# Triangle attention and triangle multiplication on one core: the output gate's constants move from POOL to PE, and the bias rows of the projections into four row tiles

## What is computed

```python
x = x + L0(gn(x))       # triangle attention, 4 heads
x = x + L1(gn(x))       # triangle multiplication
```

```python
zn   = layernorm(z) * ln_in_w + ln_in_b
a    = mask * sigmoid(zn @ a_g_w.T + a_g_b) * (zn @ a_p_w.T + a_p_b)
b    = mask * sigmoid(zn @ b_g_w.T + b_g_b) * (zn @ b_p_w.T + b_p_b)
t    = einsum('bikh,bjkh->bijh', a, b)
tn   = layernorm(t) * ln_out_w + ln_out_b
gate = sigmoid(zn @ g_w.T + g_b)
out  = gate * (tn @ z_w.T + z_b)
```

## Time and profile before

| | |
|---|---|
| median of 3 runs | 285.29 us (284.13 to 285.58) |
| the profiled execution | 284.4 us, span 282.6 us |
| mean granted clock of PE | 0.886 |
| busy | PE 80%, PE weight loads 65%, DVE 75%, ACT 74%, POOL 51% |

### The profile page before, as it was taken

How to read it: one execution, slowest core, us unless ns; L and a number is a source line. 1 busy time by engine, 2 the same in 40 slices (tenths; PEclk the granted TensorE clock), 3 DMA queues, 4 the chain that set the end, 5 groups by cost and what they waited for, 6 DMA issues and landing times.

```text
span 282.6 us, 6859 instructions
## 1 busy us (share of the span) xinstructions
PE 226.4 (80%) x2394; PEld 182.6 (65%) x2394; DVE 210.6 (75%) x368; ACT 209.2 (74%) x953; POOL 144.4 (51%) x132
## 2 busy tenths in 40 slices
PE   0589492469999999999999999999669599677930
PEld 0579230347888878888788887888459566376930
DVE  4047962357999999999999999998545739959790
ACT  0566643279999999999999999999545645569590
POOL 5400000008876777767777677766200019998081
PEclk9999668579999999999999999999958689965695
DMA  8400033534454643554445553330000000000038
GB/s 130 63 11 2 1 112 121 171 124 142 145 171 170 221 163 132 199 181 165 165 149 195 184 186 118 117 115 2 0 2 0 0 2 2 1 1 2 0 49 118
DMA packets 42389, 27.09 MB, mean 96 GB/s; under 512 B 24404, under 2 KB 42356, under 8 KB 42356
## 3 DMA queue, kind: packets, MB, share of 16 engines
q1 hardware_dynamic: 36572, 25.95, 28.8%
q10 hardware_dynamic: 5784, 0.71, 1.7%
HBM read 1.36 MB, written 1.18 MB: 9 GB/s over the span
## 4 chain that ended last, share of the span: by engine, by line
PE 31%; issue 27%; ACT 21%; DVE 12%; POOL 4%; SPq 3%; POOLq 1%; DMA 0%; DVEq 0%; ACTq 0%
ACT maps L659 17%; PE psum L1181 7%; PE psum L1060 3%; PE psum L1192 3%; PE psum L1145 2%; SPq L392 2%; DVE u_full L951 2%; PE psum L1248 2%; PE psum L1171 2%; DVE shared L991 2%; PE psum L1226 2%; PE psum L1231 2%; PE psum L1146 1%; PE psum L1148 1%; PE psum L1257 1%
## 5 line engine op out<-in xcount | busy, mean ns | idle before, releaser
L659 ACT ACTIVATE maps<-psum,neg_max 96x96 f32<-96x96 f32 x384 | 123.9, 353 | 4.9 <-DVE neg_max L928 4.1
L490 POOL TENSOR_TENSOR maps<-maps,rden 96x768 f32<-96x768 f32 x48 | 70.5, 1469 | 81.5 <-DVE rden L938 75.3
L659 ACT ACTIVATION_READ_ACCUMULATOR maps<-psum,neg_max 96x1 f32 x384 | 83.9, 219 | 0.0
L944 DVE COPY turned<-psum 96x1024 f32<-96x1024 f32 x48 | 58.5, 1219 | 8.4 <-PE psum L1181 8.4
L928 DVE TENSOR_REDUCE neg_max<-psum 96x8 f32<-96x768 f32 x48 | 45.7, 953 | 5.1 <-PE psum L1148 4.9
L1145 PE MATMUL psum<-u_st,x_stack 128*96 128x384 f32 x96 | 37.8, 394 | 10.4 <-DVE bias_lo L913 8.1
L1181 PE MATMUL psum<-ident,maps 96*96 96x96 f32 x384 | 40.0, 247 | 0.3 <-POOL maps L490 0.3
L1146 PE MATMUL psum<-bias_hi,ident_r 128*96 128x384 f32 x96 | 33.7, 351 | 0.0
L1148 PE MATMUL psum<-bias_lo,ident_r 128*96 128x384 f32 x96 | 33.4, 348 | 0.0
L1181 PEld LDWEIGHTS psum<-ident,maps 96*96 96x96 f32 x384 | 32.0, 126 | 0.5 <-POOL maps L490 0.5
L1145 PEld LDWEIGHTS psum<-u_st,x_stack 128*96 128x96 f32 x96 | 15.9, 166 | 19.8 <-issue 10.5
(11 more groups left out here) (178 smaller groups left out, 424.1 us busy)
## 6 DMA issues: line engine op xcount, KB each, us to landing
u_st<-u_split SPq DMA_DIRECT2D x96, 192.0 KB
x_stack<-shared SPq DMA_DIRECT2D x40, 96.0 KB, 2.0
maps<-in_x SPq DMA_DIRECT2D x4, 288.0 KB, 5.1
x_stack<-shared SPq DMA_DIRECT2D x4, 144.0 KB, 2.1
out_y<-maps SPq DMA_DIRECT2D x6, 96.0 KB, 3.1
out_y<-maps ACTq DMA_DIRECT2D x6, 96.0 KB, 3.4
bias_lo<-gate_sb SPq DMA_DIRECT2D x24, 12.0 KB
x_stack<-shared SPq DMA_DIRECT2D x4, 48.0 KB, 1.9
```

The source lines that it names most:

```text
L490: pool.tensor_tensor(at, at, rden[:, rows, :].unsqueeze(3).to_broadcast([N, 2, H, N]), ALU.mult).then_inc(probs_ready, 1)
L659: e = act.activation(probs[:, k % SLOTS, n, h], bank_s[r % 4][0:N, h * N:(h + 1) * N], ACT.Exp, bias=neg_max[:, r % BODY, h:h + 1], accum_ ...
L944: dve.tensor_copy(turned[0:N, j % 2].rearrange("p r x -> p (r x)"), psum[0:N, 2 * BANK:4 * BANK]).then_inc(t_ready, 1)
```

## The change

The constants leave POOL's loop. The output is now `gate * ((t centred) @ W + root * const) / root`, so `root * const` has to be added to the z quads in PSUM. That is done by PE: for quad q, position (b, f) and column j it is the root of that position times 32 constants, a matmul of the turned roots (`deviation_t`, 96 rows (b, f) by 96 columns j) with a matrix `const_rows` that spreads `z_const` to 16 (b, f) of one quad. Two quads share 32 rows, so the six matmuls lie in three row tiles of 32 rows. `const_rows` is made once by POOL (one product of 96x1024, in `u_split`, which is free behind attention) from a selection that DVE makes; the 16 operations of POOL's loop are gone.

On PE, the z quads 0 to 3 begin with a matmul of zero rows over the whole bank, then come the four z products, and the constant ends them. Quads 4 and 5 begin with the constant. The roots are turned by one transpose of PE and copied by ACT. `Z_AFTER` is 4 instead of 5; DVE waits with `Z_ORDER` for the constants, which come in the order 0, 2, 4, 1, 3, 5. The root is laid out by block, so the reciprocals are too.

The bias rows of a set use `ones_r` and `tri_b` in rows f*32 to f*32 + 31 for member f, instead of all 128 rows; SP copies the two rows of `tri_b` to the other three places by DMA, and three more memsets write the ones.

```diff
--- before.py
+++ after.py
@@ -188,8 +188,10 @@
         z_scaled = free[:, 2 * HD:3 * HD]
         z_centered = free[:, 3 * HD:4 * HD]
         beta_wide = free[:, 4 * HD:4 * HD + N]
-        gate_const = u_split[0:N, 0:2].bitcast(f32).rearrange("j s t n -> j s (t n)")[:, :, 0:GROUP * HD].rearrange(
-            "j s (b f c) -> j s b f c", f=GROUP, c=C)
+        late = u_split.bitcast(f32).rearrange("p s t n -> p (s t n)")[0:N]
+        const_rows = late[:, 0:2 * 4 * HD].rearrange("p (e x) -> p e x", e=2)
+        deviation_t = late[:, 2 * 4 * HD:2 * 4 * HD + N]
+        selected = late[:, 2 * 4 * HD + N:2 * 4 * HD + N + C]
         mask_flat = gate_sb[C:C + 2 * GROUP].rearrange("p b f c -> p (b f c)")[:, 0:BLOCKS * N].rearrange(
             "p (b n) -> p b n", n=N)
 
@@ -445,6 +452,10 @@
                     need(sp, stacked_more, 16 * COPIES * (g // 2))
                     stack(at, 2, stacked_more)
 
+            sp.wait_ge(rows_split, 1)
+            for f in range(1, GROUP):
+                sp.dma_start(tri_b[f * C:f * C + 2, :].bitcast(f32), tri_b[0:2, :].bitcast(f32)).then_inc(rows_copied, 16)
+
             for n, quads in enumerate(PIECES):
                 if quads[0]:
                     sp.wait_ge(out_ready, quads[-1] + 1 - POOL_QUADS)
@@ -503,14 +514,10 @@
                 step_pool(k)
 
             pool.wait_ge(z_prep_copied, 1)
-            for n in range(SETS):
-                product = gate_const[:, n % 2, 0:TRIO]
-                pool.wait_ge(gates_ready, 2 * n + 2)
-                constant = z_const.rearrange("j (f c) -> j f c", f=GROUP)[:, None, :, :].to_broadcast([N, TRIO, GROUP, C])
-                pool.tensor_tensor(product, gate_sb[:, trio(n)], constant, ALU.mult).then_inc(const_gated, 1)
-                pool.wait_ge(const_gated, 2 * n + 1)
-                pool.tensor_tensor(res[:, trio(n)], res[:, trio(n)], product, ALU.add).then_inc(const_gated, 1)
-                pool.wait_ge(const_gated, 2 * n + 2)
+            pool.wait_ge(selection_made, 1)
+            pool.tensor_tensor(const_rows.rearrange("p e (m c) -> p (e m) c", c=C),
+                               selected.unsqueeze(2).to_broadcast([N, C, C]),
+                               z_const[:, None, 0:C].to_broadcast([N, C, C]), ALU.mult).then_inc(const_spread, 1)
 
             def add_squares():
 
@@ -716,7 +723,10 @@
                 act.activation(tn_t[:, 4 * q:4 * q + 4, :].rearrange("p b j -> p (b j)"), banks[q % 4][:, 0:GN],
                                ACT.Copy).then_inc(tn_ready, 1)
             act.wait_ge(var_ready, 5)
-            act.activation(tok[:, 2], tok[:, 1], ACT.Sqrt).then_inc(root_ready, 1)
+            act.activation(tok[:, 2], tok[:, 1].rearrange("j b f -> j (b f)").rearrange("j (f b) -> j b f", f=GROUP),
+                           ACT.Sqrt).then_inc(root_ready, 1)
+            act.wait_ge(deviation_turned, 1)
+            act.activation(deviation_t, banks[0][0:N, 0:N], ACT.Copy).then_inc(deviation_copied, 1)
 
             act.wait_ge(root_inverted, 1)
             for q in range(POOL_QUADS):
@@ -750,6 +760,8 @@
 
             link(dve.memset(ones_r[:, :].bitcast(f32), 0.0))
             link(dve.memset(tri_b[:, :].bitcast(f32), 0.0))
+            for f in range(1, GROUP):
+                dve.memset(ones_r[f * C:f * C + 2, :].bitcast(f32), 1.0)
             link(dve.memset(ones_r[0:2, :].bitcast(f32), 1.0))
             dve.wait_ge(ident_made, 1)
             link(dve.tensor_copy(ident_r[:, :], ident[:, 0:N]))
@@ -832,6 +844,8 @@
                                          ident[:, :].rearrange("p (c f) -> p c f", f=GROUP), ALU.mult, ALU.add)
                 dve.tensor_scalar(z_scaled, tri_z[:, :, :].rearrange("p f c -> p (f c)"), gb[:, 4:5], None, ALU.mult)
                 dve.tensor_copy(beta_wide, gb[:, 5:6].to_broadcast([P, N])).then_inc(z_prepared, 1)
+                dve.tensor_reduce(selected, ident[0:N, 0:N].rearrange("p (g m) -> p m g", m=C), AX.X,
+                                  ALU.add).then_inc(selection_made, 1)
 
             def weight_stacks():
 
@@ -879,7 +893,6 @@
                 link(dve.tensor_tensor(square_total, square_total, mean_square, ALU.add))
                 dve.tensor_scalar(tok[:, 1].rearrange("j b f -> j (b f)"), square_total, 1.0 / C, EPS,
                                   ALU.mult, ALU.add).then_inc(var_ready, 1)
-                gate_z(0).then_inc(z_gated, 1)
                 dve.wait_ge(root_ready, 5)
                 dve.reciprocal(tok[:, 3], tok[:, 2]).then_inc(root_inverted, 1)
                 dve.wait_ge(root_inverted, 1)
@@ -991,10 +1004,9 @@
                 dve.tensor_tensor(ab.rearrange("k (f b) t h -> k f b (t h)", f=GROUP)[:, :, trio(n)],
                                   masked[n % MASKED], gates_ab[:, n % 2], ALU.mult).then_inc(ab_ready, 1)
             tri_statistics()
-            for q in range(1, POOL_QUADS):
+            link(scale_gates(dve, POOL_QUADS))
+            for q in range(POOL_QUADS):
                 gate_z(q).then_inc(z_gated, 1)
-            dve.wait_ge(const_gated, 2 * QUADS)
-            link(scale_gates(dve, POOL_QUADS))
             for q in range(POOL_QUADS, QUADS):
                 need(dve, gates_scaled, q - POOL_QUADS)
                 link(gate_z(q))
@@ -1065,8 +1077,8 @@
                     pe.wait_ge(z_prepared, 1)
                     z_weights = tri_z[:, :, :].rearrange("p f c -> p (f c)")
                     pe.matmul(bank_w[:, 0:HD], z_centering, z_scaled, start=True, stop=True)
-                    pe.matmul(bank_w[0:N, HD:2 * HD], ones_r[:, :],
-                              tri_b[:, None, PW:PW + C].to_broadcast([P, GROUP, C]), start=True, stop=False)
+                    pe.matmul(bank_w[0:N, HD:2 * HD], ones_r[0:C, :],
+                              tri_b[0:C, None, PW:PW + C].to_broadcast([C, GROUP, C]), start=True, stop=False)
                     pe.matmul(bank_w[0:N, HD:2 * HD], beta_wide, z_weights, start=False, stop=True).then_inc(z_prep_mm, 1)
 
             def block_transposes(q, layer, read):
@@ -1222,9 +1234,12 @@
             def project(n):
 
                 need(pe, gates_ready, 2 * (n - 1))
+                if not n:
+                    pe.wait_ge(rows_copied, 16 * (GROUP - 1))
                 for f in range(GROUP):
-                    pe.matmul(projection_bank(n, f)[0:N, 0:TRIO * PW], ones_r[:, :],
-                              tri_b[:, None, 0:PW].to_broadcast([P, TRIO, PW]), start=True, stop=False)
+                    rows = slice(f * C, (f + 1) * C)
+                    pe.matmul(projection_bank(n, f)[0:N, 0:TRIO * PW], ones_r[rows, :],
+                              tri_b[rows, None, 0:PW].to_broadcast([C, TRIO, PW]), start=True, stop=False)
                 for b in range(TRIO):
                     for f in range(GROUP):
                         at = slice(f * C, (f + 1) * C)
@@ -1250,20 +1265,46 @@
                 mm.then_inc(tri_done, 1)
 
             pe.wait_ge(tri_copied, TRI_BANKS)
-            for q in range(QUADS + Z_AFTER):
-                if q < QUADS:
-                    need(pe, tn_ready, q - 3)
-                    for n in range(4):
-                        mm = pe.transpose(banks[q % 4][:, n * N:(n + 1) * N],
-                                          tri_t[:, 4 * q + n].rearrange("p c f -> p (c f)"), ident[0:N, 0:N])
-                    mm.then_inc(block_t, 1)
-                z = q - Z_AFTER
-                if z >= 0:
-                    pe.wait_ge(tn_ready, z + 1)
-                    for n in range(4):
-                        mm = pe.matmul(z_bank(z)[0:N, n * HD:(n + 1) * HD], tn_t[:, 4 * z + n, :], z_centered,
-                                       start=True, stop=True)
+            def z_products(q):
+
+                if q < Z_EARLY:
+                    pe.matmul(z_bank(q)[0:N, :], ident_r[3 * C:P, :], bias_hi[3 * C:P].rearrange("p h k -> p (h k)")[:, None, 0:HD].to_broadcast([C, 4, HD]),
+                              start=True, stop=False)
+                pe.wait_ge(tn_ready, q + 1)
+                for n in range(4):
+                    mm = pe.matmul(z_bank(q)[0:N, n * HD:(n + 1) * HD], tn_t[:, 4 * q + n, :], z_centered,
+                                   start=False, stop=q >= Z_EARLY and n == 3)
+                if q >= Z_EARLY:
                     mm.then_inc(z_done, 1)
+
+            def z_constant(q):
+
+                rows = slice(32 * (q // 2), 32 * (q // 2) + 32)
+                mm = pe.matmul(z_bank(q)[0:N, :], deviation_t[rows, :], const_rows[rows, q % 2, :],
+                               start=q >= Z_EARLY, stop=q < Z_EARLY)
+                if q < Z_EARLY:
+                    mm.then_inc(z_done, 1)
+
+            for q in range(QUADS):
+                need(pe, tn_ready, q - 3)
+                for n in range(4):
+                    mm = pe.transpose(banks[q % 4][:, n * N:(n + 1) * N],
+                                      tri_t[:, 4 * q + n].rearrange("p c f -> p (c f)"), ident[0:N, 0:N])
```

(15 more changed lines are left out.)

13 lines of the change are left out of this document (9 added, 4 removed).

## The result

The changed kernel takes 291.14 us (median of 4 runs, 290.72 to 291.92), the kernel before 284.96 (4 runs beside it): ratio 1.0222, 95% interval 1.0185 to 1.0259. Slower, as predicted, but above the range (287.0, 282.5 to 290.0). The profiled execution took 291.92 us, its span is 290.1.

What follows compares the result with a forecast made beforehand. Waits in the last 78 us decide; in the projections PE, the two-set loop and DVE are about equally late. -4.4 + 1.7 + 4.7 = +2.0 gave 286.4 from the profiled 284.4; 287.0 was taken, range 282.5 to 290.0.

Steps and rivals of the forecast that it cites:

- Steps 1 and 2: Projections: bias rows in four row tiles and POOL's 16 constant operations gone, together 4.4 us less, bounds 1.2 and 4.8.
- under 0.4: Projections, sign of the forecast: the four bias-row matmuls of a set take under 0.4 us.
- Step 3: Second normalisation: POOL's new 96x1024 product holds up DVE's scalar variance operation, 1.7 us more, bounds 0 and 2.3.
- second rival: Second normalisation: POOL's product does not hold DVE's scalar operation, so +0.3, 285.3 us; chance 0.2.
- if L836 starts beside L518: Second normalisation, sign against the forecast: DVE's scalar variance operation starts beside POOL's new product.
- Step 4: Output stage: new PE order with zero rows and constants, net 4.7 us more, bounds 3.5 and 7; t from first transpose.
- the clock rises near t = 4.4: Output stage: PE's clock goes up about 4.4 us after the stage's first transpose.
- wrong if the six constants take over 3 us: Output stage, sign against the forecast: the six constant matmuls, expected as two rounds of 1.0 us, take over 3 us.
- First rival: Triangle products: a shorter PE gap keeps the clock at 2.4 GHz through them, 3.4 us gained, 283.6 us; chance 0.24.
- Third rival: Projections: small tiles may not bring the clock up, losing 3.4 of the 4.4 us gain, 290.4 us; chance 0.12.
- Fourth rival: Bias rows or constants: row tiles do not overlap, gain 1.2 instead of 4.4 us, 290.2 us; chance 0.05.

Runs made afterwards that it cites:

- full height: The changed kernel with each of the four 32-row matmuls of zeros made a 128-row one, overwritten by the quad's first product: 283.72 us.

## Why the prediction was wrong

- **Steps 1 and 2 (-4.4): right**, measured -4.75. Masks 1.78 apart (predicted 1.85), last product 0.96 (0.94). The four bias rows took 0.46 to 0.47 where "under 0.4" was said. The gain was put to the tiles and to POOL's absence together; row tiles alone have 1.81.
- **Step 3 (+1.7): 0 in the changed kernel, the mechanism right.** The second rival's figure came (chance 0.2), and the mark "if L836 starts beside L518" was met, but not because the scalar operation can't be held: where POOL starts 0.30 us ahead of it, it takes 1.67 us instead of 0.20, one trace. What failed is the time of POOL's start, 219.1, read from the old kernel, where the constants' matmul had 128 rows; with 32 rows ACT's copy came 0.3 us later. That 1.5 us were spared is luck, by 0.00 to 0.02 us. The sentence of the Trainium skill (SBUF — State Buffer, Who interferes with whom) that `tensor_scalar` can enter the modes in which it contends for the shared pair, and that whoever issues first keeps it for the whole instruction, agrees with the 1.67 us.
- **Step 4 (+4.7): the step that failed, +10.9.** Its sentence "the clock rises near t = 4.4" carried the time of the rise over from a kernel in which full-height products follow the transposes. The step itself put 32-row matmuls between them and didn't ask what they do to the clock. Where the clock does rise among them, the rest of the step is sound. That is best seen with four of full height in their place (*full height*): clock up at t = 6.4, first constant at 10.1 (predicted 10.6), constants 1.97 us for six (2.0), ACT's scalings at 12.1 (12.3), POOL's last add over at 20.3 (20.8), stage 281.8 - 256.24 = 25.6 us against 21.1, so +4.5 (4.7). The other 6.4 us of the +10.9 are the later rise of the clock. Without zero rows at all the stage is 24.3 us, +3.2. The mark "wrong if the six constants take over 3 us" was met: 3.74, not because the tiles fail to overlap but at 1.2 GHz.
- **First rival (clock up through the triangle products): wrong in its condition and in its price.** The gap fell to 3.08 us; with no gap the clock falls anyway, and with the clock up for over half of them the products last 10.74 us all the same. It held a chance of 0.24 and the low end of the range.
- **Third rival (clock down in the projections):** not met there, the clock rises in 230 to 232 and is 1.00 at 238 to 242. But it asked the right question, what small tiles do to the clock, for the wrong stage. Asked of the output stage it would have given the result.
- **Fourth rival (tiles don't overlap):** out, by 0.47 us for four.
- The sum: +2.0 predicted, less 1.7 (step 3), plus 6.2 (step 4), less 0.3 (steps 1 and 2) is +6.2, as measured. Step 3's miss hid part of step 4's, by luck. The range reached to 290.0 by the clock in the projections; the clock in the output stage had no case.

## What to carry to other kernels

Before a matmul is added between others, ask what it does to the clock of all that stand behind it, not only what it takes: here four matmuls of 0.46 us at 2.4 GHz, on 32 of the rows and one at a time, cost 8 us, and leaving them out (the first product starts the bank) or five unused full-height matmuls in a wait ahead of the stage gave that back. A point at which the clock rose in the old profile belongs to the old sequence of instructions and must not be carried over to a new one. The same holds for who starts first: an order of two engines that hangs on 0.3 us, as POOL's and DVE's here, must be worked out anew for the new list. And take the parts of a change one by one: the row tiles alone were worth 1.3%, hidden under a stage that cost 10.9 us.

## What the runs showed of the hardware

- TensorE's clock fell to 1.2 GHz over 96x96 products with PE 2.00 of 2.00 us busy by the records, and they were no slower for it: 64 in 10.74 us with the clock up for the first 4.6 or 5.8 us of them, and in 10.74 all at 1.2 GHz.
- With PE as busy by the records throughout, four 32-row matmuls, one ahead of each quad of full-height products, came with a rise of the clock 20.2 us behind the first transpose (291.14 us), four of 64 rows with 11.5 in the run traced (290.39), four of 128 rows and the same columns with 6.4 (283.72), none with 5.4 (283.07). In the projections, 32-row matmuls in four row tiles didn't keep it from rising (0.86 over 230 to 232).
- When it rises can differ between executions with the same list in the output stage: 13.7 and 20.2 us behind the first transpose.
- A scalar operation of DVE on SBUF (96x96, 0.20 us) took 1.67 us when POOL's product of 96x1024 had started 0.30 us ahead, and 0.20 when it started with POOL or just ahead. A reciprocal (0.75) and products with one input in PSUM ran unchanged beside POOL.
- Four float32 matmuls of 480 columns in four row tiles took 0.46 us at 2.4 GHz, 1.13 before as full-height ones.
